# Ranks and logits of a mixture of adapters from standing weights of 128 columns, and the experts' weights spread in rows

## The reference

```
logits = x @ router_W.T + router_b            # 8 experts a token
w      = softmax(logits)
a_sum  = x @ (sum of 4 blocks of 64 context rows).T     # 64 ranks a token
u[n]   = w[n] * a_sum                          # 8 x 64 = 512 values a token
upd    = sum over n of u[n] @ lora_B[n].T      # contraction over 512
h      = nan_to_num(x + 0.5 * upd, nan=0, posinf=1e4, neginf=-1e4)
```

## Time and profile before

| | us |
|---|---|
| median of 3 runs | 645.74 (645.27 to 646.33) |
| profiled execution | 646.68 |
| its span | 644.8 |
| TensorE busy | 629.9 (98%), granted clock 0.995 |
| VectorE, ScalarE, GpSimd busy | 501.5, 340.2, 268.8 (78%, 53%, 42%) |

### The profile page before, as it was taken

The page is one execution under the profiler, slowest core; times in us unless marked ns, Lnnn a source line. Parts: engine busy times, 40 slices in busy tenths (PEclk is TensorE's granted clock), DMA queues, the critical chain, the costliest instruction groups (busy, mean ns, idle before and its releaser), DMA issues.

```text
span 644.8 us, 10730 instructions
## 1 busy us (share of the span) xinstructions
PE 629.9 (98%) x3455; PEld 545.3 (85%) x3455; DVE 501.5 (78%) x907; ACT 340.2 (53%) x1000; POOL 268.8 (42%) x357
## 2 busy tenths in 40 slices
PE   9999999999999999999999999999999999999993
PEld 8988889888988889888888878888888888888883
DVE  5689995578457774577567899999999999999635
ACT  6454463123232242322167777787777787777520
POOL 0030001000020003000334556888888998888864
PEclk9999999999999999999999999999999999999998
DMA  8945695436774477722857993435354344522312
GB/s 299 376 154 177 181 301 179 158 82 213 228 268 150 110 242 240 282 64 88 239 163 252 393 355 81 146 99 168 93 149 153 126 148 120 175 79 87 111 53 99
DMA packets 103399, 114.14 MB, mean 177 GB/s; under 512 B 57008, under 2 KB 76080, under 8 KB 103344
## 3 DMA queue, kind: packets, MB, share of 16 engines
q1 hardware_dynamic: 103152, 113.20, 53.1%
q10 hardware_dynamic: 192, 0.26, 0.2%
HBM read 67.29 MB, written 46.14 MB: 176 GB/s over the span
## 4 chain that ended last, share of the span: by engine, by line
PE 91%; DMA 3%; DVE 2%; SPq 2%; issue 1%; ACT 1%; DVEq 0%; POOL 0%; POOLq 0%; ACTq 0%
PE ps L595 25%; PE ps L596 25%; PE ps L597 25%; PE ps L657 4%; PE ps L740 4%; PE ps L753 2%; PE ps L754 2%; DMA qb<-q_cols 2%; DMA x_sb<-xT 1%; PE ps L667 1%; SPq L388 1%; SPq L391 0%; PE ps L628 0%; PE ps L629 0%; PE ps L631 0%
## 5 line engine op out<-in xcount | busy, mean ns | idle before, releaser
L1244 POOL TENSOR_TENSOR u_sb<-a_sb,w_sb 128x512 f32<-128x512 f32 x16 | 19.7, 1249 | 236.8 <-DVE w_sb L872 231.9
L595 PE MATMUL ps<-wo_hi,cx_hi 128*128 128x512 f32 (+1 forms) x264 | 105.9, 401 | 0.3 <-POOL cx_lo L1283 0.3
L1173 ACT ACTIVATE s_sb<-s_sb,s_min 128x64 f32<-128x64 f32 x256 | 85.9, 339 | 30.5 <-DVE s_min L952 30.5
L597 PE MATMUL ps<-wo_hi,cx_lo 128*128 128x512 f32 (+1 forms) x264 | 101.7, 385 | 0.0
L596 PE MATMUL ps<-wo_lo,cx_hi 128*128 128x512 f32 (+1 forms) x264 | 101.6, 385 | 0.0
L595 PE MATMUL ps<-act_hi,w_hi 128*128 128x512 f32 x256 | 100.9, 394 | 0.3 <-DVE q_sb L926 0.3
L596 PE MATMUL ps<-act_lo,w_hi 128*128 128x512 f32 x256 | 99.8, 390 | 0.0
L597 PE MATMUL ps<-act_hi,w_lo 128*128 128x512 f32 x256 | 99.8, 390 | 0.0
L1138 ACT ACTIVATE act_hi<-h_t 128x512 fp32r<-128x512 f32 x32 | 20.3, 633 | 111.7 <-DVE h_t L915 111.7
L974 DVE SCALAR_TENSOR_TENSOR cx_sum<-ps,bias_c,cx_raw 64x256 f32<-64x256 f32 x128 | 61.9, 483 | 8.5 <-ACT cx_raw L1187 4.5
L1255 POOL TENSOR_TENSOR s_sb<-s_sb,s_inv 128x512 f32<-128x512 f32 x64 | 67.1, 1048 | 0.0
(11 more groups left out here) (119 smaller groups left out, 1544.5 us busy)
## 6 DMA issues: line engine op xcount, KB each, us to landing
q_cols<-q_sb SPq DMA_DIRECT2D x32, 512.0 KB, 3.6
qb<-q_cols SPq DMA_DIRECT2D x64, 256.0 KB, 4.0
x_sb<-xT SPq DMA_DIRECT2D x32, 256.0 KB, 3.1
h_rows<-hn_sb SPq DMA_DIRECT2D x64, 128.0 KB, 2.9
output_weights<-wo_sb SPq DMA_DIRECT2D x32, 256.0 KB, 2.6
z_sb<-h_rows SPq DMA_DIRECT2D x16, 512.0 KB, 5.0
out<-z_sb SPq DMA_DIRECT2D x15, 512.0 KB, 2.9
stage<-WvT SPq DMA_DIRECT2D x8, 512.0 KB, 4.7
```

Source lines behind the costliest of these rows:

```text
L595: pe.matmul(dst, lh, rh, start=(first and j == 0), stop=False)
L597: mm = pe.matmul(dst, ll, rh, start=False, stop=(last and j == n - 1))
L1173: act.activation(s_sb[c % 4][:, h, :], s_sb[c % 4][:, h, :], ACT.Exp, bias=s_min[c % 2][:, h:h + 1], scale=-1.0, accum_out=s_sum[c % 2][:, ...
```

## The change

- TensorE now holds the weights still: `a_w[0]` has 128 columns, the 64 ranks' high parts, the low parts of the first 56 ranks, and the router's 8 high columns; `a_w[1]` has the other low parts. The x chunk of 512 tokens goes through, split in `x_hi` (ScalarE) and `x_lo` (GpSimd; in batch 0 the odd chunks on VectorE), three buffers of each. That is the new stage `tokens(i, k)`: three products of 512 columns a chunk, 24 a batch.
- The result has ranks and logits in the partitions. ScalarE copies it to `a_t`; VectorE adds the low ranks, turns the logits by 32x32 blocks, makes the softmax on 32 partitions x 128 values, splits the weights, lays them in four strips and turns them back (16 steps, `ROUTE`); ScalarE copies that to `w_rows` (stage `weigh`).
- `expand` is one stage a batch: four products with a contraction over 4 rows (`choose`) spread two experts' weights over 128 partitions; VectorE multiplies by `a_t` (four products of 128x512) and makes the four low parts, ScalarE the high parts. GpSimd's multiplications and all transposes of `u` go.
- The order: the tokens of batch 0 stand behind keys 4 and ahead of the split of K5; the router of batch 0 ahead of the splits of K7 and B; `expand(0)` ahead of the split of V0. For batch 1 they stand at query groups 4 to 6 of batch 0, for batches 2 and 3 at groups 1 to 3 of the batch before.
- `k_hi` has two buffers for four batches, so `key_parts(b)` for b of 2 and 3 waits on ScalarE for the stores of all batches before (`k_stored`). The mask's load moves to behind query group 0, into the place of `u_f`.

```diff
+LOW = R - NR
+QUAD = slice(96, 128)
+ROUTER = R + LOW - QUAD.start
...
-    out += split("K", 4) + [("adapter",), ("keys", 4)] + split("K", 5, 6, 7) + split("B", 0, 1)
-    out += [("route", 0), ("keys", 5)] + split("B", 2, 3) + [("keys", 6), ("expand", 0, 0)] + split("V", 0)
-    out += [("keys", 7), ("keys_out",), ("expand", 0, 1)] + split("V", 1) + [("values", 0)] + split("V", 2) + [("mask_in",)]
+    out += split("K", 4) + [("adapter",), ("keys", 4)] + tokens(0, *range(KC)) + split("K", 5, 6)
+    out += [("route", 0), ("keys", 5)] + split("K", 7) + split("B", 0) + [("weigh", 0)] + split("B", 1) + [("keys", 6)] + split("B", 2, 3)
+    out += [("keys", 7), ("keys_out",), ("expand", 0)] + split("V", 0, 1) + [("values", 0)] + split("V", 2)
...
-                  3: split("Q", 2) + [("mask",), ("key_parts", 2)], 4: split("Q", 3) + [("key_parts", 3)], 5: [("route", 1)]}}
+                  3: split("Q", 2) + [("mask",), ("key_parts", 2)], 4: split("Q", 3) + tokens(1, 0, 1, 2),
+                  5: [("key_parts", 3)] + tokens(1, 3, 4, 5), 6: tokens(1, 6, 7) + [("route", 1), ("weigh", 1)]}}
...
-            beside[i][3] += [("route", i + 1)]
-            beside[i][5] += [("expand", i + 1, 0)]
-            beside[i][6] += [("expand", i + 1, 1)]
+            beside[i][1] += tokens(i + 1, 0, 1, 2)
+            beside[i][2] += tokens(i + 1, 3, 4, 5)
+            beside[i][3] += tokens(i + 1, 6, 7) + [("route", i + 1), ("weigh", i + 1)]
+            beside[i][5] += [("expand", i + 1)]
...
+def low_on_pool(i, k):
+    return i > 0 or k % 2 == 0
...
-        k_hi = [at(f"k_hi{k}", [P, KC, V], (AT_WO_SB if k < 2 else AT_SIGN + 4096) + 2048 * (k % 2), F32R) for k in range(NB)]
+        k_hi = [at(f"k_hi{k}", [P, KC, V], AT_WO_SB + 2048 * (k % 2), F32R) for k in range(NB)]
...
+            def tokens(i, k):                                     # TensorE
+                x_h, x_l = x_hi[k % 3][:], x_lo[k % 3][:]
...
+                pe.matmul(ps_a, a_w[0][:, k, :], x_h, start=(k == 0), stop=False)
+                pe.matmul(ps_a, a_w[0][:, k, :], x_l, start=False, stop=False)
+                pe.matmul(ps_a, a_w[1][:, k, :], x_h, start=False, stop=(k == KC - 1)).then_inc(a_mm, 1)
...
+            def expand(i):                                        # TensorE
...
+                pe.wait_ge(w_ready, i + 1)
+                wait(pe, t_ready, KC * i)
+                for j in range(RC):
+                    rows = slice(B * j, B * j + 4)
+                    pe.matmul(ps_u[j], choose[rows, :], w_rows[rows, :], start=True, stop=True).then_inc(w_mm, 1)
...
+            def expand(i):                                        # VectorE
+                def low(j):
+                    dve.wait_ge(uhi_done, RC * i + j + 1)
+                    dve.tensor_tensor(u_lo[:, j, :], u_f[j % 2][:], u_hi[:, j, :], ALU.subtract).then_inc(ulo_done, 1)
+                for j in range(RC):
+                    if j >= 2:
+                        low(j - 2)
+                        dve.wait_ge(ulo_done, RC * i + j - 1)
+                    dve.wait_ge(w_mm, RC * i + (j + 1 if j < 2 else RC))
+                    dve.tensor_tensor(u_f[j % 2][:], ps_u[j], a_t[:], ALU.mult).then_inc(u_made, 1)
+                low(2)
+                low(3)
...
             def key_parts(b):                                     # ScalarE
...
+                if b >= 2:
+                    act.wait_ge(k_stored, 32 * b)
                 act.activation(k_hi[b][:], k_full[:, b, :, :], ACT.Copy).then_inc(khi_done, 1)
...
+            def tokens(i, k):                                     # ScalarE
+                if i == 0 and k == 0:
+                    act.wait_ge(a_step, 3)
+                act.wait_ge(x_in[k], 16 * (i + 1))
+                wait(act, up_mm, KC * i)
+                if k >= 3:
+                    act.wait_ge(a_mm, KC * i + k - 2)
+                act.activation(x_hi[k % 3][:], x_sb[:, k, :], ACT.Copy).then_inc(xhi_done, 1)
             def router_exp(i):
+                act.wait_ge(a_mm, KC * (i + 1))
+                act.activation(a_t[:], ps_a, ACT.Copy).then_inc(a_copied, 1)
+                act.wait_ge(route, ROUTE * i + 5)
+                act.activation(lg[QUAD], lg[QUAD], ACT.Exp).then_inc(route_exp, 1)
+            def weigh(i):
+                act.wait_ge(route, ROUTE * (i + 1))
+                act.activation(w_rows[:], w_turned[:], ACT.Copy).then_inc(w_ready, 1)
...
+            def tokens(i, k):                                     # GpSimd
...
+                if low_on_pool(i, k):
+                    pool.wait_ge(xhi_done, KC * i + k + 1)
+                    pool.tensor_tensor(x_lo[k % 3][:], x_sb[:, k, :], x_hi[k % 3][:], ALU.subtract).then_inc(xlo_done, 1)
```

More of the change, by code:

```diff
@@ L258, in xattn_kernel @@
         u_lo = at("u_lo", [P, RC, TOK], AT_U + 8192, F32R)
[L259 removed]
+        u_f = [at(f"u_f{k}", [P, TOK], AT_U_SB + 2048 * k) for k in range(2)]
+        x_hi = [at(f"x_hi{k}", [P, TOK], AT_U + 4096 * k, F32R) for k in range(3)]
+        x_lo = [at(f"x_lo{k}", [P, TOK], AT_U + 4096 * k + 2048, F32R) for k in range(3)]
+        w_rows = at("w_rows", [P, TOK], AT_U + 12288, F32R)
+        a_t = at("a_t", [P, TOK], AT_U + 14336)
+        lg = at("lg", [P, BLOCKS, NR], AT_U)
+        w_split = at("w_split", [P, BLOCKS, RC, 4], AT_U + 2048, F32R)
+        lg_blocks = at("lg_blocks", [P, BLOCKS, B], AT_U_SB)
+        w_blocks = at("w_blocks", [P, BLOCKS, B], AT_U_SB + 2048)
+        w_turned = at("w_turned", [P, TOK], AT_U_SB)
         bound = [at(f"bound{k}", [P, TOK], AT_SIGN + 2048 * k) for k in range(2)]
@@ L674, in update @@
                     pe.wait_ge(stage_lo, PLACE["B", RC - 1] + 1)
-                if c == 0:
-                    pe.wait_ge(ulo_done, TT * (i + 1))
                 wait(pe, t_ready, m - 1)
                 cols = slice(c * P, (c + 1) * P)
-                three(ps_up[c % 2], [(b_hi[:, j, cols], b_lo[:, j, cols], u_hi[:, j, :], u_lo[:, j, :])
-                                     for j in range(RC)]).then_inc(up_mm, 1)
+                for j in range(RC):
+                    if c == 0:
+                        pe.wait_ge(ulo_done, RC * i + j + 1)
+                    mm = three(ps_up[c % 2], [(b_hi[:, j, cols], b_lo[:, j, cols], u_hi[:, j, :], u_lo[:, j, :])],
+                               first=(j == 0), last=(j == RC - 1))
+                mm.then_inc(up_mm, 1)
             def query(i, g, k):
@@ L796, in step @@
                     context(s - 6)
-            run({"keys": keys, "values": values, "route": a_and_logits, "expand": expand, "update": update,
+            run({"keys": keys, "values": values, "tokens": tokens, "expand": expand, "update": update,
                  "query": query, "pair": pair, "step": step})
@@ L852, in mask_addend @@
                 dve.tensor_tensor(mask_f[:], mask_f[:], n_set[:].unsqueeze(2).to_broadcast([P, NB, V]), ALU.add).then_inc(mask_step, 1)
+            def tokens(i, k):
+                if not low_on_pool(i, k):
+                    dve.wait_ge(xhi_done, k + 1)
+                    dve.tensor_tensor(x_lo[k % 3][:], x_sb[:, k, :], x_hi[k % 3][:], ALU.subtract).then_inc(xlo_odd, 1)
             def router(i):
-                done = 7 * i
-                bc = [P, TT, NR]
+                done = ROUTE * i
+                bc = [QUAD.stop - QUAD.start, BLOCKS, NR]
```

173 lines of the change are left out of this document (93 added, 80 removed).

## The result

The changed kernel takes 707.72 us (median of 4 runs, 706.48 to 709.04), the kernel before on the same chip 645.5: ratio 1.0963, 95% interval 1.0948 to 1.0978. The profiled execution took 706.48 us, its span is 704.7, 59.9 more than before. Of the four runs of e8_again, further down, one took 889.98 us at a granted clock of 0.654; the 659.58 given there is the median of all four, that of the other three is 658.51.

What follows compares the result with a forecast made beforehand. TensorE, busy 98% of the span, was taken as the bound. Batches 0 to 3 add 12.0+15.0+9.5+9.3 = 45.8 us, with the clock's 8 53.8; 646.7+53.8-0.9 = 699.6, stated as 699 us, range 668 to 714.

Steps and rivals of the forecast that it cites:

- rival (a): TensorE runs at half pace after every one of seven waits, 2.9 us each: 712 us; chance 0.14.
- Bound: TensorE, busy 98% of the span, has no slack: a wait put on it costs its whole length.
- Batch 0: Values 0 starts 12.0 us later, behind VectorE's router, splits and expansion; nothing is won back.
- Batch 1: Ranks and exit during batch 0's queries: 10.2+0.9+5.9+1.1-3.1 = 15.0 us.
- The 0.9 for chunks 1 and 2: In batch 1's ranks, chunks 1 and 2 follow at 1.15 us instead of 0.68: +0.9 us.
- Batches 2 and 3: Waits ahead of ranks (6.1, 5.9), at spreading (1.9) and exit (3.7): 9.5 and 9.3 us in all.
- TensorE's saving: Rank passes and transposes go, 24 products and four spreading products come: net -3.1 us a batch.
- The clock: TensorE at the lower clock level after idles of 4 to 11 us: 8 us in all (0 to 20).
- seven places: The seven idles of 4 to 11 us on TensorE, each costing from nothing to 2.9 us of clock.
- Rival (b): Chunks reach TensorE in time in batches 1 to 3: 21 us and 4 of clock, 670 us; chance 0.16.
- (c): Every chain stays hidden and 12.4 us come back: 633 us; chance 0.06.
- (d): Products on four rows or chunk products run slower than 0.227 us: 705 us or more; chance 0.04.

Runs made afterwards that it cites:

- e8_again: e7 with no low parts of x on GpSimd, mask work in batch 1's groups, batch 1's ranks and router earlier, x copies ahead of output-weight parts: 659.58 us.
- e5: Changed kernel with batch 0's four low parts of x that GpSimd made moved to VectorE: 705.82 us, ratio 1.0929.
- e2: Changed kernel with the split of V0 moved ahead of keys 7 and keys_out: 701.87 us, ratio 1.0863.
- e3: Changed kernel with key_parts(2) behind the first three chunk copies of batch 1 and key_parts(3) behind all eight: 700.63 us, ratio 1.0837.
- e1: Changed kernel with products that nobody reads put ahead of TensorE's long waits: 699.43 us, ratio 1.0833.
- e4: Changed kernel with the rank work of batches 2 and 3 two query groups later and their expansion behind query(i,1,0): 703.54 us, ratio 1.09.
- e6: Changed kernel, batches 2 and 3 rearranged: x copies and rank products as separate stages, weigh behind the exit, updates one group later, low parts on VectorE: 694.87 us.
- e7: Changed kernel with e2, e5, e6, four buffers for the keys' high parts, batch 1's copies from query group 2, its router behind group 6: 673.64 us.

## Why the prediction was right, and where its terms were off

The forecast was 699, the range 668 to 714, measured 707.72: the direction, the size and the mechanism (waits of TensorE, each as long as another engine's queue) hold. The time lies 9 us above the forecast and 0.7 above the forecast's own range (686 to 707), nearer to rival (a)'s 712 than to 699.

- **Bound.** TensorE without slack: right. The waits put on it came out in the time nearly whole (52 of the 60 us are idle time), and nothing behind won them back: phase two is as long as before.
- **Batch 0.** Values 0 expected 12.0 later, measured 13.7. The router chain was 5.9 (5.6 predicted). The rest is in the ranks: expected to start at 20.5, they did at 22.49, because GpSimd's subtraction held up the adapter's last steps. The prediction had called those steps hidden and priced them at 0.2 each; e5 shows the cause and its 2.4 us. e2 confirms the part on V0's place.
- **Batch 1.** Wait ahead of the ranks 10.2 predicted, 10.12 measured, its cause shown by e3; exit 5.9 against 6.06; `u_lo` 1.1 against 0.36. The 0.9 for chunks 1 and 2 didn't show in the kernel after: at half pace a trio takes about as long as GpSimd's subtraction (1.376 us, predicted 1.15). In e1, at full pace, it does show.
- **Batches 2 and 3.** Ahead of the ranks 6.1 and 5.9 predicted, 6.16 and 5.67 measured; spreading 1.9 against 1.98 and 1.99; exit 3.7 against 4.54 and 2.14. The cause of the first is the one predicted: the copies of x start as the last bias addition ends (rows at 200.54 and 201.17). No edit here moved the bias addition itself. What differed between the two exits wasn't traced.
- **TensorE's saving,** 3.1 us a batch predicted: too much. At full pace (e8) its busy time falls by 74.29-72.96 = 1.3 and by 2.0 twice. The count of spacings holds (24 x 0.227 and 0.44, against 8.9 before), but the first product behind a wait takes 0.34 us to the next instead of 0.227, which explains a part; the rest I didn't locate. This mis-sized term makes 1.8+1.1+1.1 = 4.0 us in batches 1 to 3.
- **The clock,** 8 us predicted in seven places: this is the term that failed in size as a term of the sum. Half pace takes 14.8 us in the trace, because each place pays 1.2 to 2.6 in place of the 1.1 that 8/7 gives, and because two more pay, the waits ahead of keys 7 and of batch 3's spreading, which the seven places didn't count. Taken away by e1 it gives 8.3 back. That this is so near to 8 is luck: the 8 was chosen between 0 and 20 with no row for a fall in mid-kernel, and the sum added it to waits of full length, which is the count, not what removing it wins.

The sum closes by the windows: 45.8 predicted; idle time in batches 1 to 3 came out 4.4 lower (18.1+12.6+12.4 predicted, 16.6+12.5+9.6 measured), the saving 4.0 smaller, half pace there 77.23-72.96 = 4.3, 2.4 and 4.9, together 11.6; batch 0 3.2 higher (15.2 against 12.0: values 0 start 1.7 later than predicted, and 1.6 are half pace behind them): 45.8-4.4+4.0+11.6+3.2 = 60.2, measured 60.1. Against the 53.8 with its 8 for the clock, half pace is thus 5.2 over and values 0 1.7; that the idle time (4.4 under) and the saving (4.0 over) cancel is luck.

Rival (b), chunks in time, and (c), all hidden, are out by the waits. (d) is out in its form: the spreading group is 0.44 and a rank trio 0.68 at full pace. (a) is the nearest: all waits of four us and more were followed by half pace, but at 1.2 to 2.6 us each, not 2.9.

## What to carry to other kernels

When the bounding engine has no slack, count a change not by what it takes off that engine but by where each helper step stands in the other engines' queues: here 3 us a batch (1.3 to 2.0 in the end) were bought with 10 to 17 us of waiting. Look for what stands between a step's inputs and the step in program order, above all an instruction that waits for a DMA: the trace names the last link (GpSimd, VectorE), the cause was a DMA two or three steps up three times: a store in the changed kernel, and loads in e4 and e6, where the edits themselves had put an output-weight part ahead of the copies. And after each repair read the waits again: e6 and e7 fell short of their expectations by stages left in the wrong place.

## What the runs showed of the hardware

- VectorE's steps with two inputs and GpSimd's subtraction don't run side by side. Steps of 64 elements took 1.3 us beside it and 0.22 without it, 1024-element splits 2.30 against 1.22, in each case about 1.1 us more, where one GpSimd subtraction takes 1.3 to 1.4. The Trainium skill ("SBUF — State Buffer", SBUF: two separate sides) has the pair of ports shared as an exclusive lock, held for a whole instruction, when VectorE reads two inputs; the trace agrees, down to the step at 19.36, which had started before GpSimd and ran 0.62, as without GpSimd. In batch 0, giving GpSimd four subtractions to relieve VectorE cost VectorE more than it gave: with them on VectorE values 0 start 2.4 us earlier (e5).
- TensorE's clock fell behind waits of 2.23, 1.99 and 2.14 us in the kernel after, yet not behind the 1.98 us ahead of batch 2's spreading in the same run (the row at 223.86), nor behind one of 2.63 us in e8 (granted clock 1.00 over that batch). Ahead of keys 7, 2.23 us cost half pace in the kernel after and 2.22 did not in e3; ahead of batch 0's ranks 1.74 did in e4 and 1.81 did not in e3. The length of the wait alone doesn't decide; what does wasn't settled. The Trainium skill ("TensorE: Matmul & The Clock Gate", Part 1: The HAM clock gate) has TensorE drop to half the clock once it has stood idle for long enough; the waits of four us and more agree; those of about 2 us went both ways.
- Four products with four rows each, on distinct row groups, take 0.44 us together with their handoff, 0.227 x 4 = 0.91 in a row. The Trainium skill ("TensorE: Matmul & The Clock Gate", Part 3: Packing small matmuls) has such products overlap; the trace agrees.
